# Last layer of a transformer chain: the first expert group's input product taken apart, and two clears moved

## What is computed

```python
scores = softmax(x @ gate_w.T)                      # 64 experts
topk_w, topk_idx = top_k(scores, 8)
w_e = zeros((N, E)).at[arange(N)[:, None], topk_idx].add(topk_w)
flat = w_e[:, inv_map]                              # 8 groups x 8 experts
scalar = flat.sum(-1)
soft = softmax(where(flat == 0, -1e9, flat), axis=-1)
xg = x[:, None, :] + einsum('ngi,ghi->ngh', soft, mask_up_w)
g = einsum('ngh,gih->ngi', xg, gate_proj_w)
u = einsum('ngh,gih->ngi', xg, up_proj_w)
d = einsum('ngi,ghi->ngh', silu(g) * u, down_proj_w)
y = einsum('ng,ngh->nh', scalar, d)
```

## Time and profile before

| | |
|---|---|
| median of 3 runs | 1546.27 us (1543.81 to 1550.5) |
| span of the profiled execution | 1552.5 us |
| PE busy | 1348.3 us, 87% |
| DVE busy | 1055.0 us, 68% |
| ACT busy | 760.9 us, 49% |
| POOL busy | 209.3 us, 13% |
| share of PE in the chain that ended last | 66% |
| mean granted TensorE clock | 0.915 |

### The profile page before, as it was taken

One profiled execution on the slowest core, in us unless ns is written; L12 is line 12 of the kernel. 1 busy time (PEld: TensorE's weight loads), 2 busy tenths in 40 slices (PEclk: granted clock), 3 DMA queues, 4 the chain that ended last, 5 costly groups with the idle time before them and its releaser, 6 DMA issues.

```text
span 1552.5 us, 21490 instructions
## 1 busy us (share of the span) xinstructions
PE 1348.3 (87%) x6917; PEld 940.6 (61%) x6925; DVE 1055.0 (68%) x2217; ACT 760.9 (49%) x1887; POOL 209.3 (13%) x221
## 2 busy tenths in 40 slices
PE   7788779968999667999998599976999999869998
PEld 4444446644444335677766489975888888744554
DVE  7999977887764697788787632226666666575564
ACT  5787723454875474655554212214666666422221
POOL 0123210010000001221111072111111111010000
PEclk9899979985986678999999789997999999968999
DMA  5222240000000200000004098845222121000100
GB/s 181 81 95 81 95 170 1 1 0 2 5 4 4 79 0 1 1 0 35 34 1 116 6 343 314 304 167 184 68 72 70 68 76 66 21 0 17 34 34 27
DMA packets 36418, 111.02 MB, mean 72 GB/s; under 512 B 4693, under 2 KB 15966, under 8 KB 30992
## 3 DMA queue, kind: packets, MB, share of 16 engines
q1 hardware_dynamic: 34464, 105.75, 19.3%
q0 software_dynamic: 1872, 4.22, 0.7%
HBM read 84.66 MB, written 26.21 MB: 71 GB/s over the span
## 4 chain that ended last, share of the span: by engine, by line
PE 66%; DVE 17%; issue 7%; ACT 5%; DMA 3%; POOL 1%; SPq 1%; DVEq 0%; ACTq 0%; POOLq 0%
PE psum L3064 6%; DVE roomA L753 5%; PE psum L2376 4%; PE psum L2715 4%; PE psum L1958 4%; PE psum L873 4%; PE psum L2663 4%; PE psum L2693 3%; PE psum L2000 3%; PE psum L2741 3%; PE psum L3074 3%; PE psum L2385 2%; PE psum L1338 2%; PE psum L1990 2%; PE psum L1370 2%
## 5 line engine op out<-in xcount | busy, mean ns | idle before, releaser
L2780 ACT ACTIVATE roomA<-psum,roomA 128x256 f32<-128x256 f32 x128 | 70.9, 559 | 92.7 <-DVE roomA L2845 92.4
L1516 DVE TENSOR_REDUCE roomB<-psum 128x2 f32<-128x512 f32 x128 | 83.9, 689 | 42.7 <-PE psum L1338 41.6
L2046 ACT ACTIVATE roomA<-psum,roomA 128x128 f32<-128x128 f32 (+1 forms) x128 | 53.2, 426 | 88.4 <-DVE roomA L2121 88.3
L3064 PE MATMUL psum<-roomA,roomB 128*128 128x512 f32 (+1 forms) x192 | 91.9, 623 | 0.3 <-ACT roomA L3171 0.3
L2515 DVE SCALAR_TENSOR_TENSOR roomA<-roomA,psum 128x512 f32<-128x512 f32 x23 | 15.8, 689 | 103.2 <-ACT roomA L2420 103.2
L1958 PE MATMUL psum<-own,roomB 128*128 128x512 f32 x160 | 75.1, 594 | 3.4 <-DVE roomA L2113 2.1
L1921 POOL TENSOR_TENSOR roomA<-roomA 128x512 f32<-128x512 f32 x40 | 50.9, 1273 | 176.9 <-DVE roomA L2114 176.9
L2715 PE MATMUL psum<-roomA 128*128 128x256 f32 x256 | 68.3, 389 | 6.0 <-DVE roomA L2857 4.4
L753 DVE TENSOR_TENSOR_SCAN roomA<-roomA 128x1024 f32<-128x1024 f32 x32 | 73.1, 2284 | 0.0
L2693 PE MATMUL psum<-roomA 128*128 128x256 f32 x256 | 65.6, 379 | 1.7 <-ACT roomA L2780 1.7
L873 PE MATMUL psum<-own,roomB 128*128 128x512 f32 x144 | 66.7, 608 | 0.0
(11 more groups left out here) (509 smaller groups left out, 3400.7 us busy)
## 6 DMA issues: line engine op xcount, KB each, us to landing
roomB<-m_w_dram SPq DMA_DIRECT2D x12, 1536.0 KB, 9.1
roomA<-m_w_dram SPq DMA_DIRECT2D x11, 1536.0 KB, 9.0
a_kv_ready<-roomB SPq DMA_DIRECT2D x32, 512.0 KB, 3.1
roomA<-a_kv_ready SPq DMA_DIRECT2D x8, 1024.0 KB, 4.8
roomA<-a_kv_ready SPq DMA_DIRECT2D x16, 512.0 KB, 4.1
roomB<-a_w_dram SPq DMA_DIRECT2D x4, 1280.0 KB, 6.3
roomB<-f_w_dram SPq DMA_DIRECT2D x8, 624.0 KB, 3.9
m_rows<-roomA SPq DMA_DIRECT2D x1, 2978.5 KB, 15.3
```

Of the source, the lines that this page charges most:

```text
L1516: dve.tensor_reduce(maxneg[:, hp // 8, :, m, hp % 8], g.bank(m).rearrange("p (q k) -> p q k", k=S), AX.X, ALU.max, negate=True).then_inc(s ...
L3064: ins = pe.matmul(g.bank(bank, rows=m), w[:, kt, at:at + m], xg[:, n % 2, kt, half * HALF:(half + 1) * HALF], start=(kt == 0), stop=(kt == ...
```

## The change

In moe3, SP loads two more tensors (group 0's mask weights transposed, and a second copy of group 0's up and gate weights), PE multiplies them to `mw` (96 x 368) after the counts, ACT copies it out of bank 3, and POOL splits it into three bf16 parts before it splits `mu`. So group 0's shift can be added after the up product: xg times W is x times W (`up_x`, f32, from x itself) plus routing times `mw` (`up_shift`, one bf16 matmul a tile). In the last layer `up_x` of three of group 0's four units stands between the steps of the head, and the fourth between turns of group 1. `shift` and `make_xg` of group 0, the four zero matmuls and their memset go; the first `down` into a bank starts it. Group 0's first two units use banks 1 to 3. The late part of the three-way split (groups 2 to 7) goes from DVE to ACT (two casts), DVE (one subtraction) and POOL (the third part). POOL clears `stack` and `hR` at the end of attn4, and both lie in another room. Rows of group 2 are turned in group 1.

```diff
         ins.then_inc(s["m3_counts"], 1)
+        ahead["tensor"](pe)
...
             pe.wait_ge(s["m3_h"], b + 1)
             if b >= 2:
                 pe.wait_ge(s["m3_y"], b - 1)
+            if b == 1:
+                pe.wait_ge(s["f5_mw_in"], 1)
...
         act.activation(b_, b_, ACT.Exp).then_inc(s["m3_exp"], 1)
+        ahead["scalar"](act)
...
             step.leave(H // 2)
+        g.f5_clear(pool)
...
     def sync(sp):
         sp.dma_start(mu, d["f5_mu"]).then_inc(s["f5_mu_in"], 16)
+        sp.dma_start(muT, d["f5_muT"]).then_inc(s["f5_w0_in"], 16)
+        sp.dma_start(w0, d["f5_w"][0, :, 0:KD * GU].rearrange("p (k n) -> p k n", k=KD)).then_inc(s["f5_w0_in"], 16)
+
+    def tensor(pe):
+        pe.wait_ge(s["f5_w0_in"], 32)
+        for kt in range(KD):
+            ins = pe.matmul(g.bank(3, GU, rows=F5_ROWS), muT[:, kt, :], w0[:, kt, :], start=(kt == 0), stop=(kt == KD - 1))
+        ins.then_inc(s["f5_mw_psum"], 1)
+
+    def scalar(act):
+        act.wait_ge(s["f5_mw_psum"], 1)
+        act.copy(mw, g.bank(3, GU, rows=F5_ROWS)).then_inc(s["f5_mw_in"], 1)
+
...
+        pool.wait_ge(s["f5_mw_in"], 1)
+        pool.tensor_copy(parts, mw).then_inc(done, 1)
+        pool.wait_ge(done, 1)
...
+        pool.tensor_tensor(parts[64:96], mw[64:96], parts[64:96], ALU.subtract).then_inc(done, 1)
+        pool.wait_ge(done, 5)
...
     def gpsimd(pool):
+        split_product(pool)
         parts, done = g.mu_parts, s["f5_mu"]
...
+    stack = wroom.take(G * NT, 3, 32, dt=BF16)
+    hR = wroom.take(2, HALF)
...
+    def clear(pool):
+        pool.memset(stack.rearrange("p n b c -> p (n b c)").bitcast(F32), 0.0).then_inc(s["f5_cleared"], 1)
+        pool.wait_ge(s["f5_cleared"], 1)
+        pool.memset(hR[32:64], 0.0).then_inc(s["f5_cleared"], 1)
+        pool.wait_ge(s["f5_cleared"], 2)
...
+    def gate_bank(n, u):
+        return u + 1 if n == 0 and u < 2 else 4 + 2 * (u % 2)
...
+        def up_x(half, rest, at):
+            w = up_weights(0)
+            for bank, col, m in tiles_of(rest, at):
+                for kt in range(KD):
+                    pe.matmul(g.bank(bank, rows=m), w[:, kt, col:col + m], g.XT[:, kt, half * HALF:(half + 1) * HALF],
+                              start=(kt == 0), stop=False)
+
+        def up_shift(half, rest, at):
+            for bank, col, m in tiles_of(rest, at):
+                ins = pe.matmul(g.bank(bank, rows=m), mw[:, col:col + m], moving[:, 0, half * HALF:(half + 1) * HALF],
+                                start=False, stop=True)
+            ins.then_inc(s["f5_up_psum"], 1)
+
         logits(pe, 1)
-        pe.wait_ge(s["f5_zeros"], 1)
-        for b in range(4):
-            pe.matmul(g.bank(b), g.identb, zeros, start=True, stop=True)
+        pe.wait_ge(s["f5_w0"], 16)
+        up_x(0, True, 1)
...
             ins.then_inc(s["f5_flat_psum"], 1)
+        up_x(0, False, 2)
+        up_x(1, True, 4)
...
         pe.wait_ge(s["f5_stack"], 1)
         pe.wait_ge(s["f5_stack_c"], 4)
         for half in range(2):
             turn_routing(0, half, 6 + half)
+        pe.wait_ge(s["f5_mw"], 5)
+        pe.wait_ge(s["f5_row"], 3)
+        pe.wait_ge(s["f5_moving"], 1)
+        spread(0, 0, 5)
+        up_shift(0, True, 1)
+        up_shift(0, False, 2)
+        pe.wait_ge(s["f5_moving"], 2)
+        spread(0, 1, 0)
+        up_shift(1, True, 4)
+        pe.wait_ge(s["f5_cb"], 1)
+        turn_routing(1, 0, 5)
+        up_x(1, False, 6)
+        up_shift(1, False, 6)
+        pe.wait_ge(s["f5_moving"], 3)
+        turn_routing(1, 1, 5)
         pe.wait_ge(s["f5_mu"], 5)
-        pe.wait_ge(s["f5_row"], 3)
-        pe.wait_ge(s["f5_moving"], 2)
-        for kt in range(KD):
-            shift(0, kt, 4 + 2 * kt)
+        pe.wait_ge(s["f5_cb"], 2)
+        pe.wait_ge(s["f5_read"], 1)
+        pe.wait_ge(s["f5_moving"], 4)
+        shift(1, 0, 0)
+        pe.wait_ge(s["f5_read"], 2)
+        shift(1, 1, 2)
+        spread(1, 0, 5)
         pe.wait_ge(s["f5_xg"], 1)
-        for half in range(2):
-            spread(0, half, 4 + half)
-        for n in range(G):
+        pe.wait_ge(s["f5_h"], 2)
+        down(0, 0, False)
+        pe.wait_ge(s["f5_cb"], 3)
+        spread(1, 1, 5)
+        for n in range(1, G):
             pe.wait_ge(s[f"f5_w{n % SLOTS}"], 16 * (n // SLOTS) + 16)
...
+            act.activation(th[0:m, u % 2], g.bank(gate_bank(n, u), rows=m), ACT.Tanh, scale=0.5).then_inc(s["f5_th"], 1)
 
         for half in range(2):
             turned(0, half, 6 + half)
-        for half in range(2):
-            spread(0, half, 4 + half)
-        for n in range(G):
+        spread(0, 0, 5)
+        tanh(0, 0)
+        spread(0, 1, 0)
+        tanh(0, 1)
+        turned(1, 0, 5)
+        act.wait_ge(s["f5_soft"], 1)
+        act.copy(part(False, 0), thrice(False, soft)).then_inc(s["f5_high"], 1)
+        turned(1, 1, 5)
+        tanh(0, 2)
+        act.wait_ge(s["f5_left"], 1)
+        act.copy(part(False, 1), thrice(False, left)).then_inc(s["f5_middle"], 1)
+        spread(1, 0, 5)
+        tanh(0, 3)
+        spread(1, 1, 5)
+        for n in range(1, G):
             tanh(n, 0)
-            if n == 0:
-                turned(1, 0, 5)
+            if n == 1:
+                turned(2, 0, 5)
             tanh(n, 1)
-            if n == 0:
-                turned(1, 1, 5)
+            if n == 1:
+                turned(2, 1, 5)
             if n + 1 < G:
...
     def gpsimd(pool):
-        pool.memset(stack.rearrange("p n b c -> p (n b c)").bitcast(F32), 0.0).then_inc(s["f5_cleared"], 1)
-        pool.wait_ge(s["f5_cleared"], 1)
-        pool.memset(hR[32:64], 0.0).then_inc(s["f5_cleared"], 1)
-        pool.wait_ge(s["f5_cleared"], 2)
...
+        pool.wait_ge(s["f5_left"], 1)
+        pool.wait_ge(s["f5_middle"], 1)
+        pool.tensor_tensor(part(False, 2), thrice(False, left), part(False, 1), ALU.subtract).then_inc(s["f5_stack"], 1)
...
-        softmax(True)
+            return dve.tensor_tensor(a, a, of.unsqueeze(2).to_broadcast(list(a.shape)), ALU.mult)
+
+        step(softmax(True))
         dve.wait_ge(s["f5_cleared"], 2)
-        stacked(True)
-        softmax(False)
+        step(dve.tensor_copy(part(True, 0), thrice(True, soft)))
+        step(dve.tensor_tensor(left[:, some(True)], soft[:, some(True)], part(True, 0)[:, :, 0], ALU.subtract))
+        step(dve.tensor_copy(part(True, 1), thrice(True, left)))
+        dve.tensor_tensor(part(True, 2), thrice(True, left), part(True, 1), ALU.subtract).then_inc(s["f5_stack"], 1)
+        softmax(False).then_inc(s["f5_soft"], 1)
...
-        for n in range(G):
+        unit(0, 0)
+        unit(0, 1)
+        dve.wait_ge(s["f5_soft"], 1)
+        dve.wait_ge(s["f5_high"], 1)
+        dve.tensor_tensor(left[:, some(False)], soft[:, some(False)], part(False, 0)[:, :, 0], ALU.subtract).then_inc(s["f5_left"], 1)
+        make_xg(1, 0, 0)
+        make_xg(1, 1, 2)
+        unit(0, 2)
+        unit(0, 3)
+        for n in range(1, G):
             unit(n, 0)
```

More of the change, by code:

```diff
@@ L2926, in ffn5_ahead @@
     g.mu_parts = room.take(F5_G * D, dt=BF16, rows=F5_ROWS)
+    muT, w0 = room.take(KD, F5_ROWS), room.take(KD, GU)
+    mw = room.take(GU, rows=F5_ROWS)
+    g.mw_parts = room.take(GU, dt=BF16, rows=F5_ROWS)
     g.routed_rows = room.take(P, dt=BF16, rows=32)
@@ L2975, in ffn5 @@
     of_group = room.take(G * NT)
-    stack = room.take(G * NT, 3, 32, dt=BF16)
     weT = room.take(TOK, rows=E)
@@ L3061, in up @@
             w = up_weights(n)
-            for bank, at, m in ((4, 2 * P, UP_AT + REST),) if rest else ((6, 0, P), (7, P, P)):
+            for bank, at, m in tiles_of(rest, 4 if rest else 6):
                 for kt in range(KD):
@@ L3256, in softmax @@
         def softmax(first):
-            some = slice(0, FIRST) if first else slice(FIRST, G * NT)
-            a, kept, of = soft[:, some], present[:, some], of_group[:, some]
-            step(dve.tensor_scalar(kept, flat_[:, some], 0.0, LEAST, ALU.not_equal, ALU.max))
+            a, kept, of = soft[:, some(first)], present[:, some(first)], of_group[:, some(first)]
+            step(dve.tensor_scalar(kept, flat_[:, some(first)], 0.0, LEAST, ALU.not_equal, ALU.max))
             if first:
```

99 lines of the change are left out of this document (47 added, 52 removed).

## The result

| | before | after | ratio (95%) |
|---|---|---|---|
| first comparison, median of 18 and 18 | 1547.18 us | 1537.94 us | 0.9928 (0.991 to 0.9945) |
| second, on another occasion, median of 23 and 12 | 1545.08 us | 1537.05 us | 0.9961 (0.9932 to 0.999) |
| span of the profiled execution | 1552.5 us | 1534.8 us | |

The change makes the kernel faster: by 9.2 us by the medians and 11.1 us (8.5 to 13.9) by the ratio of the first comparison, by 8.0 and 6.0 us (1.5 to 10.5) in the second. Forecast were 10.1. The sum is right, but two of its terms are not: the head (from attn4's last output projection to P) gained 15 to 17 us where the forecast had 11.1, and the way from moe3 to that projection, forecast to lose 1.0 us, lost about 5.7.

What follows compares the result with a forecast made beforehand. PE was taken to bound the kernel, without idle time from 1414 on, behind a chain of waits at half clock. 11.9 - 0.8 (clock) - 1.0 (block) = 10.1 us off 1546.27 gave 1536.2; range for 8 in 10, 1531.0 to 1541.5.

Steps and rivals of the forecast that it cites:

- What bounds it: From 1414 on PE has no idle time and full clock, so a head ending earlier moves the end by as much.
- Norm and clears: Last layer's norm: L195 and L203, 2.1 us late beside POOL's memset, return to 0.17; only 0.81 us comes off the path.
- The block at attn4's end: POOL's moved memsets hold up DVE's L2851, and PE behind it, by 1.0 us (bounds 0 and 1.5).
- The first product: up_x(0, rest) fits the 4.0 us gap behind the logits with 0.3 to spare; 1.73 us taken from behind.
- From t0 to P: From the routing's turning (1394.2) to unit (1, half 1 rest): 17.06 us work plus 4.5 waits, ending at 1415.8 against 1427.67.
- The fall of the clock: A second fall before unit (1, half 1 rest) cost 1.65 us; half, 0.8, is taken off the gain.
- Casts and POOL's third part: ACT's casts of 1152 elements take 1.3 us each at most, covered; POOL's part 2.3, needed some four us later.
- (a): Rival: POOL's third part takes 9.2 us, not 2.3, so group 2's turning waits some 4.5 us: 1540.7; chance 0.11.
- (c): Rival, slower: the same POOL operation costs still more, deciding from about 16 us on; at 20 us, 1550; chance 0.04.
- (b): Rival: clock stays at 1.2 GHz through the products and mixed work behind; gain about 0, 1546.3; chance 0.08.
- (d): Rival: PE waits longer for ACT, giving back what the products saved at turned and spread: 1539.6; chance 0.11.
- so I take 0; uncovered it is 3.7: In moe3 POOL's split adds at most 3.7 us ahead of the scatter; ACT needs the buffer five blocks later, so 0.

Runs made afterwards that it cites:

- after_timed: The changed kernel, no edit, profiled and timed again: median 1537.05 us, ratio to before 0.9961.
- first_late: The changed kernel with the first x product moved from behind the logits to behind the flat products: second half's logits to routing's turning 22.6 us, changed kernel 16.2 to 16.4.
- clears_later: The changed kernel with POOL's two clears held back until attn4's last turned result: moe3's first scatter to attn4's last output projection 469.54 us, 470.38 without the edit.
- best: The changed kernel with POOL's product split behind moe3's last scatter and its clears behind attn4's last turned result: median 1533.08 us, ratio to before 0.9921.
- clock_first: The kernel before, with the first x product run behind the logits and thrown away: routing's turning 1.2 us earlier, unit (1, half 1 rest) 0.9 us earlier.
- clock_all: The kernel before, with all x products ahead of the routing's turning run at their new places and thrown away: unit (1, half 1 rest) 4.1 us earlier.
- warm: The changed kernel with nine thrown-away matmuls in PE's idle gaps of the norm: routing's turning 36.31 us behind attn4's last output projection, 33.28 without them.

## Why the prediction was right, point by point

- **What bounds it.** Right. All time won ahead of P arrives at the end: P to the last unit was 110.97 to 110.99 in thirteen executions.
- **Norm and clears.** L195 and L203 took 0.17 us each, as said, and PE is late next: the transposes at 1368.81 follow the logits with no idle time. Where all of the first half's logits ran at half clock, as before, the transposes started 3.44 us behind them (after_timed, first_late, clears_later) against 4.46 before (1371.44 - 1366.98), so about 1.0 comes off where the forecast had 0.81. What a single execution gained varies more, 0.2 to 1.9 us at the second half's logits, since the clock fell at another point of the norm in each execution: between 11.5 and 13.5 us behind W in after, and in best between 9.1 and 11.1,

```profile
1356.00:1358.00 2.00, 1.35 (x8) 0.95 (x8) 1.75 (x9) 1.14 (x4) 0.00 (x0) 0.82 0.00 0
1358.00:1360.00 2.00, 1.30 (x6) 1.33 (x7) 1.73 (x11) 0.84 (x2) 0.00 (x0) 0.50 0.00 0
```

  which accounts for nearly all of the range of W to t0 in after, 33.2 to 35.0.
- **The block at attn4's end.** Right: 1.0 forecast, 1.2 measured, by the mechanism named. DVE's first step took 2.44 us and ended 0.15 behind the first memset, the second ended 0.15 behind the second, and PE stood idle for 1.00 us.
- **The first product, "nothing gained or lost here".** This is the first of two steps that failed. The product costs nothing, but it lets PE run on for 3 to 4 us behind the logits, and the clock rises in it. The forecast put the rise 4.7 us into the *later* products, with L3034 and L3041 still at half clock. t0 was forecast at 1394.2 - 1355.37 = 38.8 us behind W; it came at 33.2 to 35.0. Of after's 5.5 us, 5.58 - 3.04 = 2.5 are the turning of weights and the flat products at full clock, 7.6 - 5.4 = 2.2 the later products; the remaining 0.8 lies in the norm. first_late, in which the early product is missing, gives P 63.3 behind W, near the forecast's 60.4. Both rises of the earlier trace rows came under unbroken matmuls; I did not carry this over to the four records that directly follow the logits' sixteen.
- **ACT's order.** The rows of before, which are empty ahead, read from the exponentials (L3158) over turned (L3165) and spread (L3171) to tanh (L3178):

```order
L3158 ACTIVATE roomA<-roomA 128x128
L3158 ACTIVATE roomA<-roomA 128x384
L3165 CAST roomA<-psum 96x512 x2
L3171 COPY roomA<-psum 128x512 x2
L3178 ACTIVATE roomA<-psum 48x512
L3165 CAST roomA<-psum 96x512
L3178 ACTIVATE roomA<-psum 128x512
```

- **From t0 to P.** Right in the sum: 17.06 of work and 4.5 of waits made 21.6; measured 22.1. But the waits behind t0 were 0.54, 0.76, 0.57, 0.34 and 0.94 us, 3.15 together, and the rest, 18.9, is more than the work was priced at. The two errors nearly cancel. The fall of the clock was given half a chance at 1.65 us; it came in three of nine profiles, at 1.2 to 1.3.
- **Casts and POOL's third part.** Right: casts 1.17 and 1.14, POOL 2.37 (2.3 forecast), nobody waits. Rivals (a) and (c) fall with it:

```profile
1397.38 2.37 POOL L3314 TENSOR_TENSOR roomB<-roomA,roomB 128x1152 bf16<-128x1152 f32 x1 [11.12 <-ACT roomB L3279]
```

- **Rivals (b) and (d).** (b) had the clock stay down through the products: not seen in any of the nine profiles with the new head, though in one of them, first_late, without the early product, it was at 0.50 from 1377 to 1395, most of the way to t0 (1399.81). (d) falls: no wait for ACT between t0 and P is over 0.94.
- **moe3, "so I take 0; uncovered it is 3.7".** Wrong, the second step that failed. I asked only whether a later first scatter holds up ACT (it came 3.4 us later behind M, and ACT did not wait for it), and not what else POOL's later operations meet. It is the mechanism that I had weighed for the clears. The Trainium skill, page "SBUF — State Buffer", section "Who interferes with whom", says that a VectorE instruction with two SBUF inputs contends with a GpSimd instruction that reads SBUF, and that the lock is exclusive. The rows of L2509 and L2510, which have two such inputs, agree, to 0.06 us; L2512, a cast with one input, is not in that sentence, and ended 0.04 us behind POOL's operation all the same. Measured cost: 4.4 us, about half of it the wait and half the clock.
- **The sum.** 11.9 - 0.8 - 1.0 = 10.1 stands against, in the lengths of the table, a head of 15.2 to 16.9 and M to W of -5.7 (470.1 against 464.4, the mean of before, clock_first and clock_all, the block's 1.0 included). The forecast's head was 11.1 and its M to W -1.0. The total is right because a gain of 4 to 6 us and a loss of 4.4 to 4.7 that I had both left out cancel: that the number came out is luck, though the mechanisms of most terms hold. (In the chances, nine tenths of 0.66 and a third of 0.22 are 0.67 for faster, not 0.70.)

## What to carry to other kernels

Ask of every piece of matmul work put into an idle gap not only whether it fits but what clock the groups behind it will then have: here two matmuls that cost nothing were worth 6.2 to 6.4 us by their place, and in warm the clock fell again behind a gap of 2.3 us that was left open. Ask of every operation put on POOL what it pushes later on POOL, and lay DVE's small steps beside that: a step of 0.2 us can take as long as the POOL operation that it meets. Where executions differ by more than the change, compare stages between fixed points.
